# Expert layer of a graph network on one core: three buffers for ReLU outputs and results, the residual sum on GpSimd, the first expert begun with four row tiles, and row gathers that wait for the feature rows alone

## What is computed

```python
probs = softmax(xn @ gate_w + gate_b)          # xn = layernorm(x); 8 experts
idx   = argmax(probs, axis=-1)                 # one expert for each node
pos   = rank of the node among those of its expert;  kept = pos < 977
buf[idx, pos] = xn                             # rows of each expert, in order
hmid  = relu(buf @ w1 + b1)                    # 256 -> 1024, per expert
ybuf  = hmid @ w2 + b2                         # 1024 -> 256
y     = ybuf[idx, pos] * (prb * kept)
y     = nan_to_num(y, nan=0.0, posinf=10000.0, neginf=-10000.0)
return x + y
```

## Time and profile before

| | us |
|---|---|
| median of 3 runs | 2598.12 (2594.09 to 2600.07) |
| profiled execution | 2596.97 |
| its span, first to last instruction | 2595.3 |
| stage of edges and attention | about 50 to 2065 |
| gate stage | 2065.5 to 2162.8 |
| expert stage | 2162.8 to the end |

### The profile page before, as it was taken

How to read it: one execution, slowest core, us unless ns; L and a number is a source line. 1 busy time by engine, 2 the same in 40 slices (tenths; PEclk the granted TensorE clock), 3 DMA queues, 4 the chain that set the end, 5 groups by cost and what they waited for, 6 DMA issues and landing times. The chain is left out here.

```text
span 2595.3 us, 33207 instructions
## 1 busy us (share of the span) xinstructions
PE 1927.2 (74%) x8866; PEld 1534.0 (59%) x8866; DVE 1245.3 (48%) x3250; ACT 797.4 (31%) x1559; POOL 1793.1 (69%) x1908
## 2 busy tenths in 40 slices
PE   8588887666776766776777777766666676999997
PEld 6355555455555555655555555655444575888886
DVE  6334323344444453443544444443322385878886
ACT  5222222133333333332333333332000054444442
POOL 6577777777777777777777777777777602666665
PEclk9799999899888898888888888888877756999998
DMA  7433333333333333333333333333333444222220
GB/s 223 129 104 106 106 106 106 105 105 105 105 106 104 106 104 106 106 105 105 105 106 105 105 106 106 104 105 106 105 105 105 131 147 117 63 79 67 86 70 8
DMA packets 128069, 270.88 MB, mean 104 GB/s; under 512 B 33608, under 2 KB 71460, under 8 KB 127770
## 3 DMA queue, kind: packets, MB, share of 16 engines
q0 software_dynamic: 82992, 221.52, 29.9%
q1 hardware_dynamic: 44906, 47.32, 5.6%
HBM read 244.15 MB, written 27.35 MB: 105 GB/s over the span
## 5 line engine op out<-in xcount | busy, mean ns | idle before, releaser
L776 POOL DMA_INDIRECT ring<-node_rows,src_chunk x1563 | 1484.7, 950 | 493.1 <-issue 475.8
L800 PE MATMUL p_item<-ring,sel 128*128 x3512 | 1018.0, 434 | 536.8 <-SPq L757 534.3
L800 PEld LDWEIGHTS p_item<-ring,sel 128*128 128x128 f32 x3512 | 708.0, 214 | 774.7 <-issue 684.0
L1063 DVE TENSOR_TENSOR acc<-acc,p_item 128x256 f32 (+1 forms) x439 | 184.2, 419 | 826.7 <-PE p_item L800 822.4
L1045 DVE SCALAR_TENSOR_TENSOR sel<-dst_chunk,nbase,p_col 128x512 f32<-128x512 f32 x439 | 326.7, 744 | 57.1 <-issue 38.8
L1934 PE MATMUL e_y<-w2h,hTh 128*128 128x256 f32 x512 | 150.8, 295 | 3.6 <-DVE hTl L1643 3.6
L1389 POOL DMA_INDIRECT rows<-node_features,slot_row x64 | 72.3, 1130 | 114.5 <-DMA out_dram<-res 95.4
L1934 PE MATMUL e_y<-w2h,hTl 128*128 128x256 f32 x512 | 145.4, 284 | 0.0
L1934 PE MATMUL e_y<-w2l,hTh 128*128 128x256 f32 x512 | 145.3, 284 | 0.0
L957 ACT ACTIVATE x1T<-p_t,col_ln1b,col_ln1g 128x128 f32<-128x128 f32 x98 | 39.5, 453 | 343.9 <-PE p_t L833 343.9
L1141 DVE SCALAR_TENSOR_TENSOR kf<-p_q,ke 128x256 f32<-128x256 f32 x49 | 20.8, 425 | 203.7 <-ACT ke L940 203.7
(11 more groups left out here) (257 smaller groups left out, 2921.9 us busy)
## 6 DMA issues: line engine op xcount, KB each, us to landing
ring<-node_rows,src_chunk POOLq DMA_INDIRECT x1563, 2.7
w1raw<-in_w SPq DMA_DIRECT2D x8, 1024.0 KB, 5.0
w2raw<-in_w SPq DMA_DIRECT2D x8, 1024.0 KB, 6.7
res<-in_x SPq DMA_DIRECT2D x7, 896.0 KB, 9.9
node_features<-res SPq DMA_DIRECT2D x3, 1554.0 KB, 7.5
out_dram<-res SPq DMA_DIRECT2D x3, 1536.0 KB, 10.6
node_rows<-acc SPq DMA_DIRECT2D x4, 1024.0 KB, 4.9
node_rows<-acc SPq DMA_DIRECT2D x3, 512.0 KB, 5.0
```

Of the source, the lines that this page charges most:

```text
L776: nc.gpsimd.indirect_dma_start(ring[:, c % RING // U, c % U, :], None, table, bass.IndirectOffsetOnAxis(src_chunk[:, c:c + 1], 0)).then_in ...
L800: mm = pe.matmul(p_item[bank(i)][:, 0:C], sel[:, i % SELR, u, :], rows[:, u, :], start=(u == 0), stop=(u == U - 1), skip_group_check=True)
L1063: nc.vector.tensor_tensor(a, a, p_item[bank(j)][:, 0:C], ALU.add).then_inc(added, 1)
```

## The change

1. `NBUF` = 3: `hbuf`, `yv`, `low`, `big`, `finite`, `total` and `oo` get three buffers, tile t (or slice j) in t % 3, with three semaphores `sent` for the stores; waits for a free buffer look three tiles back (`last_use`), not two. `hbuf` moves to memory that the gate stage has left, and `one_lo` changes its place.
2. `total` leaves DVE's `classify` and becomes a third tensor_tensor of each tile on POOL, ahead of the sum `low` + `big`, waiting for `yv` alone.
3. In expert 0 PE transposes tiles 0 to 3, then makes product (slice 0, half 0), transposes 4 and 5, makes (slice 1, half 0), transposes 6 and 7, and goes on with (0, 1), (1, 1) and the rest in the old order. ReLUs follow that order.
4. `x2_out` gets a semaphore of its own, `dma_x2`; the gathers of expert 0 wait for the five transfers of feature rows alone, and POOL waits for `dma_x2` behind them, ACT ahead of its experts. The semaphores `arrived` are now shared with the first stage, and the waits add what that stage left in them.

```diff
-NOUT = 2 * (len(RB) - 1)
+NOUT = len(RB) - 1
+CROWS = [0, 9, 17, 25, 33, 41, NBLK]
+NBUF = 3
...
-        yb, yv = sb("yb", [P, 2, C], st=st), sb("yv", [P, 2, C], st=st)
+        yb, yv = sb("yb", [P, 2, C], st=st), sb("yv", [P, NBUF, C], st=st)
...
+        def halves(e):
+            if isinstance(e, int) and e == 0:
+                return [(0, 0), (1, 0), (0, 1), (1, 1)] + [(j, h) for j in range(2, FT) for h in range(2)]
+            return [(j, h) for j in range(FT) for h in range(2)]
...
+        def last_use(T, t):
+            return T - NBUF + 1 if t >= NBUF else T - RT + next(i for i in range(RT - 1, -1, -1)
+                                                                if i % NBUF == t % NBUF) - t + 1
...
-                             res[:, blocks(gi), 0:C]).then_inc(dma_out, 16)
+                             res[:, blocks(gi), 0:C]).then_inc(dma_x2, 16)
...
             pool.wait_ge(dma_out, 16 * NOUT)
             load_rows(0)
+            pool.wait_ge(dma_x2, 16 * NOUT)
...
+                    pool.wait_ge(y_ok, T + 1)
+                    wait(pool, o_ok, last_use(T, t))
+                    nc.gpsimd.tensor_tensor(total[0:r, s, :], yv[0:r, s, :], rows[0:r, e % 2, t, 0:C], ALU.add
+                                            ).then_inc(pool_st, 1)
                     pool.wait_ge(inf_ok, T * 2 + 2)
-                    nc.gpsimd.tensor_tensor(low[0:r, t % 2, :], low[0:r, t % 2, :], big[0:r, t % 2, :], ALU.add
+                    nc.gpsimd.tensor_tensor(low[0:r, s, :], low[0:r, s, :], big[0:r, s, :], ALU.add
                                             ).then_inc(pool_st, 1)
-                    pool.wait_ge(pool_st, T * 2 + 1)
-                    wait(pool, sent[t % 2], T // 2 * 16)
+                    pool.wait_ge(pool_st, T * 3 + 2)
+                    wait(pool, sent[s], 16 * (e * len(range(s, RT, NBUF)) + t // NBUF))
...
-                    V.tensor_tensor(total[0:r, t % 2, :], yv[0:r, t % 2, :], rows[0:r, u, t, 0:C], ALU.add
-                                    ).then_inc(fin_ok, 1)
...
-                        wait_apart(s, lo_ok, e * FT + j - 1, dma_fb, 32)
+                    wait_apart(s, lo_ok, e * FT + max(j - NBUF + 1, 0), dma_fb, 32)
...
-                    wait(s, o_ok, e * RT + t - 1)
+                    wait(s, o_ok, last_use(e * RT + t, t))
...
+                    if first and c in (1, 2):
+                        for t in range(2 * c + 2, 2 * c + 4):
+                            transposes(0, t)
+                    if first and c == 2:
+                        t_.wait_ge(pads, 4 if CAPE > CAP else 2)
...
-            for t in range(RT):
+            for t in range(4):
                 transposes(0, t)
-            t_.wait_ge(pads, 4 if CAPE > CAP else 2)
             all_experts(t_, expert)
```

More of the change, by code:

```diff
@@ L116, in build @@
         gathered = [sem(f"gathered{i}") for i in range(RING // U)]
+        arrived = [sem(f"arrived{i}") for i in range(RT)]
         dma_out = sem("dma_out")
@@ L232, in prepare @@
         dma_x = [sem(f"dma_x{i}", st) for i in range(NG)]
-        dma_crow = [sem(f"dma_crow{i}", st) for i in range(NC)]
+        arrived = g["arrived"]
         dma_tab = sem("dma_tab", st)
@@ L1268, in tail @@
         w2h, w2l = late("w2h", [P, FT, C], F32R), late("w2l", [P, FT, C], F32R)
[L1269 to L1272, removed]
+        finite = late("finite", [P, NBUF, C], I32)
+        low, big = late("low", [P, NBUF, C]), late("big", [P, NBUF, C])
+        total, oo = late("total", [P, NBUF, C]), late("oo", [P, NBUF, C])
+        assert NBUF * CAPE * 4 <= XT * 2 * CH * P * 4 + 2 * RGM * P * 2
+        hbuf = nc.alloc_sbuf_tensor_at("hbuf", [P, NBUF, CAPE], F32, offset=hbuf_at)
         p_t = [ps(f"e_t{i}", [P, 4, P], st) for i in range(2)]
@@ L1281, in tail @@
         d_w1, d_w2 = sem("d_w1", st), sem("d_w2", st)
-        arrived = [sem(f"arrived{t}", st) for t in range(RT)]
-        sent = [sem(f"e_sent{i}", st) for i in range(2)]
+        sent = [sem(f"e_sent{i}", st) for i in range(NBUF)]
+        dma_x2 = sem("dma_x2", st)
         (xe_ok, tr_ok, bh_ok, bl_ok, f1_ps, r_ok, hi_ok, lo_ok, f2_ps, yb_ok, y_ok, pool_st, inf_ok, fin_ok, o_ok,
@@ L1425, in _ @@
                     load_rows(e + 2)
-            for q in range(2):
-                pool.wait_ge(sent[q], 16 * EXP * RT // 2)
+            for q in range(NBUF):
+                pool.wait_ge(sent[q], 16 * EXP * len(range(q, RT, NBUF)))
         @block.vector
@@ L1772, in expert @@
             def expert(e, u, more):
-                for j in range(FT):
-                    for h in range(2):
-                        wait_apart(s, f1_ps, e * 2 * FT + 2 * j + h + 1, dma_fb, 32)
-                        wait_apart(s, lo_ok, e * FT + j - 1, dma_fb, 32)
-                        nc.scalar.activation(hbuf[:, j % 2, h * NH[0]:h * NH[0] + NH[h]],
-                                             p_f[(2 * j + h) % 4][:, 0:NH[h]], ACT.Relu,
-                                             bias=fb1_sb[:, bass.ds(e, 1), j]).then_inc(r_ok, 1)
-                    if 1 <= j < 1 + PC:
+                for c, (j, h) in enumerate(halves(e)):
+                    wait_apart(s, f1_ps, e * 2 * FT + c + 1, dma_fb, 32)
+                    wait_apart(s, lo_ok, e * FT + max(j - NBUF + 1, 0), dma_fb, 32)
+                    nc.scalar.activation(hbuf[:, j % NBUF, h * NH[0]:h * NH[0] + NH[h]], p_f[c % 4][:, 0:NH[h]],
+                                         ACT.Relu, bias=fb1_sb[:, bass.ds(e, 1), j]).then_inc(r_ok, 1)
+                    if h == 1 and 1 <= j < 1 + PC:
                         high_w2(e, j - 1)
-                    if more and j == FT - 2:
+                    if more and h == 1 and j == FT - 2:
                         normalise(e + 1, 1 - u, 0)
```

79 lines of the change are left out of this document (39 added, 40 removed).

## The result

| | before | after |
|---|---|---|
| median of 12 runs each, us | 2598.26 | 2594.37 |
| lowest to highest | 2594.09 to 2601.9 | 2591.89 to 2596.53 |
| ratio, 95% interval | | 0.9984, 0.9976 to 0.9992 |
| span of the profiled execution | 2595.3 | 2594.7 |

The change makes the kernel 3.9 us faster, 0.16%: within the 0.2% that I had called no difference. The interval leaves out 1, so a small gain is there all the same, which I had said could not be told from none. The two spans differ by less, because the edge stage, which the change does not touch, ended 3.0 us later in the profiled execution of after (first gate instruction at 2068.74 against 2065.70).

A forecast was written before the change was run, and what follows sets the result against it. The prediction took a POOL and DVE loop, not PE, to bound the expert stage. Start -2.4, periods and expert 3 +0.5, end +1.2 gave -0.7 on 2596.97, so 2596.3; with the median's offset considered it said 2596, range 2578 to 2611.

The forecast's parts named there:

- case A: Whole kernel: terms as summed, expert period within 0.5 of the old; 2596 us, own range 2591 to 2600, chance 0.40.
- DVE's part: Expert stage, from the end of oo(6) to the next expert's first bias addition: 22.0 us, 0.7 longer than before.
- The bound: Expert stage: a loop over POOL and DVE sets the period, oo(6) + 21.3 us before the change; PE has slack.
- Three buffers: Second layer: store landing leaves POOL's cycle, nothing left of 39.1 us of waits; third hbuf worth nothing by itself.
- POOL's tile, 3.65 and 4.05: Second layer with total on POOL: 3.65 us a tile, 4.05 for tiles 2 to 4 beside w1l; five tiles 19.45.
- Expert 3's stall, -1.5: Expert 3: a third yv removes a stall of some 1.5 us beyond the usual period, counted once.
- The start, -2.4: Expert 0: earlier gathers and first products bring its first bias addition 2.4 us earlier, bounds 0 to -3.
- The end, +1.2: Last expert, no w1l: oo(7) ends at 30.65 to 31.1 us after the mark, not 29.6, adding 1.2.
- B: Second layer: POOL gets its turn whenever it asks, tile 3.5, period 48.3; 2579 us, chance 0.25.
- C: Expert stage: PE becomes the bound, 3.1 us less per expert; 2574 us, chance 0.05.
- D: Second layer: DVE holds up POOL's sums, tile 4.3, period 52.8; 2611 us, slower from tile 4.15; chance 0.22.
- E: Expert 0: its new order doesn't help, the layer ends as before; 2598.5 us, chance 0.08.

The follow-up runs named there:

- x1_total_dve: The changed kernel with a small edge-stage index edit and the residual sum back on DVE, three buffers kept; 2950.56 us, ratio 0.9950 to the kernel before.
- x6: The changed kernel with DVE's four w1l quarters of experts 1 to 7 cut from 512 to 8 columns; 2584.58 us beside 2600.91 for the kernel before.
- x4_two_buffers: The changed kernel with two buffers in all places, the sum left on POOL; mean period 51.38 us.
- x3_wait_both: The changed kernel with expert 0's gathers waiting for the output rows too; node list to first mark 40.99 us.
- x7: The kernel of x1_total_dve with the residual sum left out altogether, selecting yv in place of total; 2563.18 us, period 46.39.
- x9: The kernel of x7 with DVE selecting into low first and POOL then adding the residual rows once; 2569.57 us, ratio 0.9880 to the kernel before.
- x2: The changed kernel with expert 0's transposes and products in the old order, early gathers kept; node list to first mark 40.05 us.
- x8: The kernel of x1_total_dve with one of the first layer's three products (w1l times bTh) left out; 2568.82 us, period 48.07.
- c1_before_edit: The kernel before with only the edge-stage edit that masks two indices; ratio 1.0025 to the kernel before, periods 50.46 us.

## Why the prediction was right, and which terms were off

The forecast 2596 with case A holds: after took 2594.37 in the median. Two signs of being wrong that I had named are touched: single tiles of expert 2 lie outside 3.65 to 4.1 (3.48 and 4.23, the mean of five is 3.88), and DVE's part is 21.5 and not 22.0.

- **The bound.** Right: the period is oo(6) + DVE's part, in the mean 29.24 + 21.42 before, 28.98 + 21.50 after and 26.14 + 21.50 in x1_total_dve. The third buffer's 3.0 us are all in oo(6).
- **Three buffers, "nothing left" of the landing.** Right; no wait for a store is left in after. What the prediction did not ask is what they are worth alone: 3.0 per expert, and 2.9 of it went back into the move. That the sum came out near nothing is two terms of some 20 us each over seven periods that cancel; the prediction had their difference, not the two. One late store at tile 5 holds 3.06 of the waiting. The mean of 3.95 was arithmetically sound and hid this.
- **POOL's tile, 3.65 and 4.05.** Right in the sum, which is what oo(6) rests on: in expert 2 tiles 2 to 6 take 3.90, 4.04, 4.23, 3.77 and 3.48, together 19.42, forecast 19.45, and oo(6) ends at 28.60, forecast 28.75. total was forecast at 0.70 and took 0.73 in the mean. The collision had the right size in these tiles (1.05 by x6, forecast 1.2), but it falls on low and not on total.
- **DVE's part.** Direction right, size off. Behind oo(6) DVE's part was to be 22.0, 0.7 longer; its mean is 21.50 (20.9 to 22.0), and before it was 21.09 with expert 3 left out, so 0.4 longer. This and expert 3 are why the periods gave -1.2 and not +0.5.
- **Expert 3's stall, -1.5.** The number came (52.03 to 50.20, -1.8), the reason is not borne out. x4_two_buffers, with only two yv buffers, has no long expert 3 (51.36 beside 51.65 and 50.85), while every kernel with three buffers and the sum on DVE keeps one (49.48 beside 47.72 and 47.80 in x1_total_dve, where DVE waits 1.17 for `hbuf`). In these traces the stall goes with the move of the sum, not with the third yv; what causes it stays open.
- **The start, -2.4.** Undersized: -3.8 (42.70 to 38.92). The gathers were to begin 1.0 earlier and began 1.5 earlier: I gave POOL 0.75 behind the node list, the delay that the earlier trace rows show behind a DMA, and behind DVE it is 0.50 - 0.22 = 0.3. x3_wait_both shows this part alone, 1.5 to 2.3. The first product came 9.8 after the node list, forecast 10.1, and the third at 16.7, forecast 18.1; this is the rest.
- **The end, +1.2.** Measured +0.6 from the last mark on: oo(7) at 30.21, forecast 30.65, before 29.60.
- **The rivals.** B would need tiles of 3.5; x6 has 3.4 to 3.8 (3.67 on average) and 48.8, so B is near what the kernel would be without the w1l collision. C named PE as the next bound at 3.1 less; x1 has that period (47.6) with PE not the bound: x7 and x9 go on to 46.4. D: total's mean is 0.73, not over 0.85; the collisions fall on low (0.93), not on total. D's threshold of 4.15 a tile leaves out the 0.7 that D itself adds behind oo(6): with it the period there is 9.3 + 20.75 + 22.0 = 52.05, and seven of them lose some 10 and not 6. E: made unlikely by the starts of x2 and x3, as above.

In sum, the forecast was right with terms wrong in the same direction (periods 1.7 too high, start 1.4, end 0.6 too high), 3.7 together, less 0.8 of gate stage that is not the change's: the traces give -3.6 for a forecast of -0.7.

## What to carry to other kernels

Do not move work onto the engine whose cycle sets the period, even if it has long waits: a wait that another part of the same change removes is not free time. Read a cycle tile by tile before taking its mean; one late transfer beside a large load can be half of the waiting. And before asking which engine should do an operation, ask whether the formula needs it: folding the residual sum into the one that was there anyway, with three buffers, brought 31 us; moving it, with the same buffers and the same start, 4.

## What the runs showed of the hardware

- The 1 MB load delays a small store issued 0.6 us behind it from 2.6 to 4.9 us.
- PE's clock falls after a stretch in which PE waits, also in the middle of dense work, and the periods with such a dip are longer. Experts 1 and 2 of after differ in this (stretches of one period each):

```profile
2254.30:2305.40 51.10, 48.09 (x307) 44.24 (x306) 38.98 (x72) 24.77 (x48) 40.08 (x40) 0.97 0.23 68
2305.40:2355.40 50.00, 46.98 (x307) 42.68 (x306) 39.93 (x72) 24.68 (x48) 39.45 (x40) 1.00 0.28 85
```

  Inside the first of them, the 4 us in which PE waits and the next 4:

```profile
2298.30:2302.30 4.00, 1.93 (x15) 1.90 (x15) 3.93 (x6) 1.54 (x3) 3.09 (x4) 0.93 0.52 102
2302.30:2306.30 4.00, 4.00 (x25) 4.00 (x25) 2.33 (x4) 0.34 (x1) 2.15 (x2) 0.64 1.03 290
```

  Three of after's seven periods have 0.97 and are 50.56 to 51.09, the four with 1.00 are 50.00 to 50.20 and, with POOL's gap of 1.89 in it, 50.69. How much of the difference is the clock and how much the wait ahead of it is not shown. Removing PE work (x8) brought more such dips, 0.90 to 0.96 per period.
- The kernel before takes 2598 us on one chip and 2965 on another. By the traces of before and c1_before_edit, all of the difference lies ahead of the gate stage, which starts 400 us later, in the edge stage with its 1563 gathers; the periods agree within 0.4%.
- POOL's indirect store takes 1.01 (median) in experts 2 to 5 of before and in nearly all of x9, and 1.25 in the other experts of before and in after and x4, for the same transfer; in x1_total_dve both occur in turn. Nothing in these traces says why; at eight tiles it is 2 us per expert of POOL's time.
